# Reordering GpSimd's queue in a fused graph-layer kernel: gathers issued one step early, between the subtractions

## The reference, cut to what matters

```python
xn = _layernorm(x)
# graph part: per node, logits from the rows of src and dst, softmax over 4 heads, weighted sum of the dst row
xt = (xn @ weight).reshape(-1, 4, 64)
alpha = softmax(leaky_relu((xt[row] * attn_l).sum(-1) + (xt[col] * attn_r).sum(-1), 0.01), axis=1)
gnn = broadcast(einsum('nh,nhd->nd', alpha[:n], xt[col[:n]]))
# mix part: linear attention, then a two-layer MLP on [xn, msg], with layer norms
h = relu(concatenate([xn, _layernorm(msg @ Wm)]) @ W1) @ W2
x = x + gnn + xn + _layernorm(h)
# ffn part: shared MLP plus the best 2 of 4 experts, weighted by a softmax over the gates
x = x + shared(_layernorm(x)) + gated_experts(_layernorm(x))
```

## Time and profile before

| | us |
|---|---|
| median of 3 runs | 1589.8 (1586.72 to 1592.46) |
| the profiled execution, its own time | 1592.46 |
| its span (first to last instruction) | 1590.6 |
| busy: TensorE / VectorE / ScalarE / GpSimd | 1455.4 / 1174.3 / 832.5 / 997.9 |
| mean granted TensorE clock, share of full speed | 0.962 |

### The profile page before, as it was taken

How to read it: one execution, slowest core, us unless ns; L and a number is a source line. 1 busy time by engine, 2 the same in 40 slices (tenths; PEclk the granted TensorE clock), 3 DMA queues, 4 the chain that set the end, 5 groups by cost and what they waited for, 6 DMA issues and landing times.

```text
span 1590.6 us, 27346 instructions
## 1 busy us (share of the span) xinstructions
PE 1455.4 (91%) x9090; PEld 1310.3 (82%) x9090; DVE 1174.3 (74%) x2812; ACT 832.5 (52%) x1466; POOL 997.9 (63%) x973
## 2 busy tenths in 40 slices
PE   5799999779999999999999999999999999999986
PEld 4799999668888888888888888888888888888875
DVE  4678778557778777887778777787777877778772
ACT  3355555235564456545565455654556446564553
POOL 4567776466766676567665666666776567765542
PEclk9899999789999999999999999999999999999998
DMA  5333332111111011001110011100111001110000
GB/s 162 109 109 111 109 109 95 21 27 28 40 34 27 20 39 39 27 22 30 39 36 24 27 31 39 35 24 23 36 39 34 25 20 39 39 33 27 4 16 20
DMA packets 46514, 70.39 MB, mean 44 GB/s; under 512 B 25738, under 2 KB 30471, under 8 KB 46483
## 3 DMA queue, kind: packets, MB, share of 16 engines
q1 hardware_dynamic: 30482, 56.58, 10.9%
q0 software_dynamic: 16000, 13.43, 3.9%
HBM read 43.77 MB, written 26.00 MB: 44 GB/s over the span
## 4 chain that ended last, share of the span: by engine, by line
PE 66%; DVE 16%; ACT 5%; issue 5%; DVEq 2%; SPq 1%; DMA 1%; POOL 1%; POOLq 1%; ACTq 0%
PE psum L211 19%; PE psum L212 19%; PE psum L213 19%; DVE top_e L1095 7%; PE psum L355 5%; DVE qf L995 2%; ACT e_hi L748 1%; SPq L276 1%; ACT relu L747 1%; DMA xb<-in_x 1%; PE psum L509 1%; ACT qf L731 1%; PE psum L595 1%; PE psum L515 1%; PE psum L638 1%
## 5 line engine op out<-in xcount | busy, mean ns | idle before, releaser
L211 PE MATMUL psum<-w_hi,h_hi 128*125 128x256 f32 x600 | 172.6, 288 | 4.6 <-DVE h_lo L1208 4.6
L212 PE MATMUL psum<-w_lo,h_hi 128*125 128x256 f32 x600 | 170.1, 284 | 0.0
L213 PE MATMUL psum<-w_hi,h_lo 128*125 128x256 f32 x600 | 169.8, 283 | 0.0
L1329 POOL DMA_INDIRECT xg<-table_xt,idx x100 | 125.4, 1254 | 56.1 <-issue 56.1
L1335 POOL TENSOR_TENSOR h_lo<-relu,h_hi 128x1000 fp32r<-128x1000 f32 x50 | 123.9, 2480 | 50.0 <-ACT h_hi L748 50.0
L1331 POOL DMA_INDIRECT ag<-table_al,idx x100 | 121.2, 1212 | 30.5 <-issue 30.5
L752 ACT ACTIVATE scaleT<-psum 128x500 fp32r<-128x500 f32 x27 | 15.9, 589 | 230.5 <-PE psum L509 230.5
L211 PE MATMUL psum<-z_hi,w_hi 128*128 128x500 f32 x300 | 121.5, 405 | 2.3 <-DVE z_lo L1156 2.3
L211 PE MATMUL psum<-xT_hi,w_hi 128*128 128x500 f32 x300 | 120.7, 402 | 2.4 <-DVE xT_lo L988 2.4
L212 PE MATMUL psum<-xT_lo,w_hi 128*128 128x500 f32 x300 | 118.0, 393 | 0.0
L1335 POOL TENSOR_TENSOR e_lo<-relu,e_hi 128x1000 fp32r<-128x1000 f32 x50 | 115.8, 2343 | 3.3 <-ACT e_hi L748 2.7
(11 more groups left out here) (236 smaller groups left out, 5013.7 us busy)
## 6 DMA issues: line engine op xcount, KB each, us to landing
xb<-in_x SPq DMA_DIRECT2D x50, 500.0 KB
table_xt<-xts SPq DMA_DIRECT2D x25, 507.8 KB
out<-xmid SPq DMA_DIRECT2D x25, 500.0 KB
xg<-table_xt,idx POOLq DMA_INDIRECT x100
ag<-table_al,idx POOLq DMA_INDIRECT x100
w_raw<-in_L_mix_W SPq DMA_DIRECT2D x1, 1024.0 KB
w_raw<-in_L_mix_W SPq DMA_DIRECT2D x1, 512.0 KB
w_raw<-in_L_ffn_eW SPq DMA_DIRECT2D x1, 512.0 KB
```

The costliest lines, as they stand in the source:

```text
L211: pe.matmul(out, wh, xh, start=first, stop=False)
L212: pe.matmul(out, wh, xl, start=False, stop=False)
L213: return pe.matmul(out, wl, xh, start=False, stop=last)
L1329: pool.indirect_dma_start(xg[par][:, j, :], None, table_xt.ap(), bass.IndirectOffsetOnAxis(idx[par][:, 1, j:j + 1], 0)).then_inc(S[f"gath{ ...
```

## The change

All of it is in GpSimd's queue. All eight transfers for group `i+1` are now issued in step `i`: tiles 0 and 1 after `base` as before, tile 2 between the two `e1_lo` subtractions, tile 3 after the second one, ahead of `rs_x`. Nothing is gathered at the head of a step. Group 0 is gathered before step 0, and group 1 in step 0, group 2 in step 1 (there all eight together, since stage c is missing). `rs_y` moves ahead of `s2_lo`. The added parameter of `gathers` isn't used in it.

```diff
-            def gathers(par, tiles):
+            def gathers(v, par, tiles):
...
-                ahead = a and more and b
-                if a:
-                    if not isinstance(i, int) or i > 1:
-                        gathers(par, (2, 3))
-                    else:
-                        pool.wait_ge(S[f"idx{par}"], 2 * dma16(i, par))
-                        gathers(par, range(T))
...
-                    if ahead:
+                    if a and more:
                         pool.wait_ge(S[f"idx{1 - par}"], 2 * dma16(i + 1, 1 - par))
...
-                    if ahead:
-                        gathers(1 - par, (0, 1))
+                if a and more:
+                    if not b:
+                        pool.wait_ge(S[f"idx{1 - par}"], 2 * dma16(i + 1, 1 - par))
+                    gathers(i + 1, 1 - par, (0, 1))
...
                         low(e1_lo[:, 2 * n:2 * n + 2, :], relu[n][:], e1_hi[:, 2 * n:2 * n + 2, :], "e1_lo")
+                        if n == 0 and a and more:
+                            gathers(i + 1, 1 - par, (2,))
                 if a and more:
+                    gathers(i + 1, 1 - par, (3,) if c else (2, 3))
                     rs_of_x(i + 1, 1 - par)
+                if b:
+                    if due(i - 1):
+                        pool.wait_ge(S["y"], i - 1)
+                    rstd(LY, "mv_y", i, "rs_y")
                 if c:
...
                     low(s2_lo[:], relu[2][:, 0, :], s2_hi[:], "s2_lo")
-                if b:
-                    if due(i - 1):
-                        pool.wait_ge(S["y"], i - 1)
-                    rstd(LY, "mv_y", i, "rs_y")
...
             enter_phase2(pool)
+            pool.wait_ge(S["idx0"], 2 * dma16(0, 0))
+            gathers(0, 0, range(T))
             phase2(0, 0, b=False, c=False)
```

## The result

The changed kernel takes 1625.84 us (median, 1625.17 to 1626.26) against 1589.37 before: a ratio of 1.0231, 95% interval 1.0218 to 1.0245. Forecast was 1554, range 1528 to 1604. The span of its profiled execution is 1624.3 us.

The account below looks back on a forecast made before the run. It took L1095, held by GpSimd's `e_lo`, with TensorE idling behind it, as the bound. 1592.46 + 12.1 - 48.4 = 1556.2 us for the profiled execution, 1553.5 against the median, stated as 1554; range 1528 to 1604.

Parts of the forecast that it names:

- What bounds the kernel: VectorE's L1095 is held until GpSimd's `e_lo` ends; TensorE then idles 2.65 us ahead of L509 in 22 steps.
- Rival D: L1095 is long for another reason, so the change only costs its 12.1 us: 1602 us, chance 0.04.
- L1095 free at the end of the first `e_lo`, L509 2.3 us earlier: L1095 ends 2.31 us earlier, leaving 0.34 us idle ahead of L509; the clock's fall there is taken as gone.
- The margin of L1114 to the second `e_lo`: VectorE's L1114 starts 1.28 us before the second `e_lo` and stays free, with 0.34 us to spare.
- rival A: VectorE's L1114 is held by the second `e_lo`, L509 comes 1.2 us later than before: 1636 us, chance 0.17.
- The new wait at L638: TensorE's output block waits 1.5 us for `s2_lo`, which ends at 753.1 behind GpSimd's later work.
- the term for `rs_x`: In GpSimd's sum up to `s2_lo`, `rs_x` costs 3.28 us, of which up to 0.5 may go.
- No price in the sum for the clock behind this wait: The 48.1 us step left out a clock fall at the output block, called open at 1.2 us a step.
- rival B: The clock keeps falling, now behind the wait for `s2_lo`: 1.2 us a step, 1580 us, chance 0.10.
- Steps 0 and 1: Eight more transfers ahead of `rs_x` in step 0 expose 12.1 us once; in step 1 they cost nothing.

Follow-up runs that it names:

- `s2_lo` between: The changed kernel with `s2_lo` moved between tile 3's transfers and `rs_x`: 1555.3 us, ratio 0.9791 to the kernel before.
- step 0: The changed kernel with group 1's eight transfers moved behind `rs_m` of the first step: 1612.7 us, ratio 1.0147 to the kernel before.
- `rs_y` alone: The kernel before with only `rs_y` moved ahead of `s2_lo`: 1583.5 us, ratio 0.9965 to the kernel before.
- tile 3 at the head: The changed kernel with only tile 3's transfers put back to the head of the next step: 1526.8 us, ratio 0.9612 to the kernel before.

## Why the prediction was wrong, point by point

- **What bounds the kernel: right.** L1095 is held by GpSimd's `e_lo`, and L509 and the clock hang behind it. With L1095 free the kernel is 5.7% faster. Rival D is out: in the changed kernel L1095 ends at 755.02 (751.91 + 3.11), with the first `e_lo` at 754.98, though by the profile it started 0.72 us before it.
- **L1095 free at the end of the first `e_lo`, L509 2.3 us earlier: right.** The idle time is 0.50 us for 0.34 forecast, and the clock behind L509 stays up, as taken.
- **The margin of L1114 to the second `e_lo`: right.** It starts at 756.62, 1.30 us before the second `e_lo` (forecast 1.28), and takes 0.18 us. L1100's two copies, the first 0.18 us into a gather, take 0.17 us each. So rival A, which named a time near the measured one, 1636, did so by a mechanism that did not occur.
- **The new wait at L638: the first step that failed, in the term for `rs_x`.** The place and the chain to `s2_lo` were right; the sum put `rs_x` at 2.8 to 3.3 us and it is 4.58 in step 9. Two pieces: the drain directly behind a gather costs 1.7 us and not 0.81, shown by `s2_lo` between. And the small instructions, of which the forecast struck out up to 0.5 us because VectorE's two-input work would be over by then, cost 0.9 more than their shortest (0.73 and 0.59 us while L1208, which has two inputs in SBUF, ran from 766.56). From the shortest `rs_x` of the kernel before, 2.78 us, these make 2.78 + 0.9 + 0.9 = 4.58. The forecast looked at the two-input work that had been beside them before and not at what comes next in VectorE's queue. That L1208 is the cause is read from the timelines, where they become short when it is over; no run took it away. `rs_x` and `rs_y` together take 6.3 to 6.4 us in 21 of the 22 steps, for 5.0 in the sum. TensorE asks where the forecast had it (15.5 us behind the first `e_lo`, for 15.3), and so the wait became 2.8 us in the mean in place of 1.5.
- **No price in the sum for the clock behind this wait: the second step that failed, and the dearer one.** The sum took the clock as up, and rival B had the fall as its own case, at 1.2 us a step and a chance of 0.10. Behind 2.7 to 3.1 us of wait the clock fell in 21 of 22 steps, and the block costs 1.5 us more. The prediction argued against B with "1.5 us, not 2.65" and so hung this step on the one before it. No run has a wait of 1.5 us at L638, so whether that argument was good stays open; 1.0 us leaves the clock up.
- **Steps 0 and 1: right.** TensorE's wait for the first `row_n` of step 0 is 17.57 us for 5.45 before, 12.12 more (12.1 forecast). At L509 of step 2 it is 10.65, mostly since that step's own idle time is already 2.1 us shorter.

Per step, from 48.92 at full clock: less 2.15 at L509, plus 2.8 at L638, plus about 1.5 for the block, plus 0.15 in the matmuls between L509 and L638 (11.15 us busy for 10.99): 51.2, measured 51.29. Before it was 50.30, since there the clock fell too. 21 steps of 1.0 us, 10.7 at the start and 2.2 at the end make the 33.7 us between the two spans. Against the 48.1 of the forecast, 1.3 of the 3.2 us missed are the longer wait, 1.5 the clock.

The 1555 us of `s2_lo` between are close to the forecast's 1554, but that is chance and bears nothing out: that run has no wait at L638 and loses its time at `row_n` and `mT_lo` instead.

What stays open: which waits bring the clock down. The length of the last wait alone doesn't settle it. A wait of 1.43 us late in step 26 leaves it up in the traces of all ten kernels. In step 25, waits of 0.8 us at L612 and 1.0 to 1.1 at L638 follow each other closely; the clock is down behind them in the changed kernel and in the run "step 0", and up in the runs "`rs_y` alone" and "tile 3 at the head". Timeline and stretch of the changed kernel in step 26, its stretch in step 25, and that of "`rs_y` alone" in step 25:

```profile
1600.08 0.46 PE L211 MATMUL psum<-s_hi,w_hi 128*128 128x500 f32 x1 [1.43 <-ACT e_hi L748]
1600.08:1604.88 4.80, 4.31 (x18) 3.28 (x19) 4.15 (x10) 2.38 (x4) 3.68 (x2) 1.00 0.00 0
1573.88:1578.88 5.00, 4.51 (x19) 4.21 (x20) 4.71 (x10) 0.93 (x2) 0.00 (x0) 0.50 0.01 3
1527.56:1532.56 5.00, 4.04 (x31) 3.83 (x32) 4.71 (x10) 0.93 (x2) 0.00 (x0) 1.00 0.01 3
```

Open too: why behind 2.65 us it fell in 17 of 22 steps and not in 5, and most of the 0.33 us a step by which `rs_y` alone is faster.

## What to carry to other kernels

When work is moved along an in-order queue, price the whole tail behind its new place up to the next thing another engine asks for, each instruction at what it costs with its new neighbours, not at its old mean. A hold that hurts is better avoided by moving the holder (one `e_lo`, nothing added to the tail) than by putting other work into the gap. When a change makes a new wait, put the fall of the clock behind it into the sum, as a price of its own with its own chance: here a wait of 1.0 us cost 1.1 us, and one of 2.8 cost 4.3.

## What the runs showed of the hardware that was not expected

- GpSimd's drain directly behind an indirect transfer costs more: 1.5 to 2.0 us ahead of `rs_x` in 21 of 22 steps of the changed kernel, and 0.81 with the 1.28 us of `s2_lo` between. Step 0 of the kernel before had it already, 1.68 us.
- The hold between VectorE and GpSimd goes both ways, and small work can pay several times its own length for it: an instruction of four elements a row took 0.73 us in place of 0.24 on GpSimd beside VectorE's L1208. It ended at 767.30, the first of L1208's two instances at 767.21. This agrees with the Trainium skill, "SBUF — State Buffer", section "Who interferes with whom", which has the loser blocked until the other ends.
- VectorE can be held before GpSimd's subtraction starts by the profile: where a gather stands ahead of `e_lo`, L1095 was held when it started 0.73 us before it, and other instructions with two SBUF inputs were free at 0.93 us and more.
- VectorE isn't let in between two subtractions that follow each other directly (L1095 was held through both `e_lo`, 5.25 us), and it is when a gather stands between them: L1095 went on 0.04 us after the first one's end.
- A cast of 16 elements on VectorE that started 0.73 us into a gather ran until that gather's end (748.04 to 748.49, the gather ends at 748.52), 0.45 us for 0.17. That is where rival A put its doubt. But work at a gather's start lost nothing: in the changed kernel L1097's cast, 0.07 us before one, and L1100's copies, 0.18 us and more into it, take 0.17 us each in all 22 steps. No run has a cast that starts just after a gather does.
